# An earlier L1 tail in the head of batch 2, with its weight steps, rows and CA product moved

## The reference, cut to what matters

```
x = x + L0(x)      # L0: sum of 3 gated MLPs per batch, 256 -> 1024 -> 256: one shared, 2 chosen experts
x = x + L1(x)      # L1: one expert: down(silu(up(x)+bu) * (gate(x)+bg)) + bd, 256 -> 512 -> 256
x = x + L2(x)      # L2: x @ (sum_g y_g weight_g * mask)^T + bias
x = x + L3(x)      # L3: x @ W_base^T + b_base + 2 * (low-rank x @ A^T B^T weighted by w)
# x is (4, 512, 256): four batches of 512 rows. L0 MLP: gelu(x@g) * (x@u) @ d
```

## Time and profile before

| | |
|---|---|
| median of 3 runs | 494.5 us (494.38 to 494.57) |
| the profiled execution | 495.4 us |
| its span, first to last instruction | 493.7 us |
| mean granted TensorE clock | 0.993 |
| PE busy | 485.0 us (98%) |
| DVE busy | 376.4 us (76%) |
| ACT busy | 265.4 us (54%) |
| PE's share of the chain that ended last | 92% |

### The profile page before, as it was taken

One profiled execution on the slowest core, in us unless ns is written; L12 is line 12 of the kernel. 1 busy time (PEld: TensorE's weight loads), 2 busy tenths in 40 slices (PEclk: granted clock), 3 DMA queues, 4 the chain that ended last, 5 costly groups with the idle time before them and its releaser, 6 DMA issues.

```text
span 493.7 us, 6911 instructions
## 1 busy us (share of the span) xinstructions
PE 485.0 (98%) x2260; PEld 404.1 (82%) x2260; DVE 376.4 (76%) x647; ACT 265.4 (54%) x426; POOL 29.8 (6%) x51
## 2 busy tenths in 40 slices
PE   7999999999999999999999799999999999999997
PEld 6887888888888888888888588888888888888897
DVE  3869878977536588986987868898887577867766
ACT  4555644645446444655544646676666363636452
POOL 1820300000000200000000001000000000020000
PEclk8999999999999999999999989999999999999999
DMA  7778898258320432424380052304049220230001
GB/s 220 153 153 225 201 204 200 64 150 148 89 64 0 123 113 66 127 72 122 87 169 0 1 161 75 100 29 126 3 101 198 88 64 2 64 108 0 2 0 44
DMA packets 113812, 48.33 MB, mean 98 GB/s; under 512 B 66344, under 2 KB 112560, under 8 KB 113776
## 3 DMA queue, kind: packets, MB, share of 16 engines
q1 hardware_dynamic: 111328, 42.74, 34.6%
q0 software_dynamic: 2448, 5.15, 4.0%
HBM read 45.77 MB, written 2.10 MB: 97 GB/s over the span
## 4 chain that ended last, share of the span: by engine, by line
PE 92%; DVE 4%; ACT 1%; issue 1%; DMA 1%; SPq 0%; DVEq 0%; ACTq 0%
PE bank_a L1491 8%; PE bank_a L1492 8%; PE bank_a L1493 8%; PE bank_b L1492 8%; PE bank_b L1491 8%; PE bank_b L1493 8%; PE out L1515 6%; PE out L1519 6%; PE out L1516 6%; PE tail L1492 2%; PE tail L1493 2%; PE tail L1491 2%; PE tail L1515 2%; PE tail L1516 2%; PE tail L1519 2%; PE bank_a L1767 2%
## 5 line engine op out<-in xcount | busy, mean ns | idle before, releaser
L646 ACT ACTIVATE hid_hi<-hid 128x512 fp32r<-128x512 f32 x92 | 58.1, 632 | 93.8 <-DVE hid L905 57.2
L638 ACT ACTIVATE hid<-bank_a 128x512 f32<-128x512 f32 x80 | 47.6, 595 | 57.4 <-PE bank_a L1493 56.3
L913 DVE TENSOR_TENSOR hid_lo<-hid,hid_hi 128x512 fp32r<-128x512 f32 x92 | 63.2, 687 | 14.0 <-ACT hid_hi L646 14.0
L905 DVE SCALAR_TENSOR_TENSOR hid<-bank_b,mine,hid 128x512 f32<-128x512 f32 x64 | 47.6, 744 | 31.2 <-PE bank_b L1493 29.7
L893 DVE TENSOR_TENSOR w_lo<-raw,w_hi 128x768 fp32r<-128x768 f32 x59 | 56.0, 950 | 0.0
L1492 PE MATMUL bank_a<-x_lo,w_hi 128*128 128x512 f32 x118 | 46.0, 390 | 0.0
L1491 PE MATMUL bank_a<-x_hi,w_hi 128*128 128x512 f32 x118 | 46.0, 390 | 0.0
L1493 PE MATMUL bank_b<-x_hi,w_lo 128*128 128x512 f32 x118 | 45.9, 389 | 0.0
L1493 PE MATMUL bank_a<-x_hi,w_lo 128*128 128x512 f32 x118 | 45.9, 389 | 0.0
L1491 PE MATMUL bank_b<-x_hi,w_hi 128*128 128x512 f32 x118 | 45.9, 389 | 0.0
L1492 PE MATMUL bank_b<-x_lo,w_hi 128*128 128x512 f32 x118 | 45.9, 389 | 0.0
(11 more groups left out here) (327 smaller groups left out, 1131.9 us busy)
## 6 DMA issues: line engine op xcount, KB each, us to landing
raw<-in_L_cond_skill_gate SPq DMA_DIRECT2D x32, 256.0 KB, 2.9
raw<-in_L_cond_skill_up SPq DMA_DIRECT2D x32, 256.0 KB, 3.1
raw<-in_L_cond_skill_down SPq DMA_DIRECT2D x64, 128.0 KB, 3.2
raw<-in_L_cond_shared_down SPq DMA_DIRECT2D x22, 128.0 KB, 3.6
raw<-in_L_cond_shared_gate SPq DMA_DIRECT2D x10, 256.0 KB, 2.9
raw<-in_L_cond_shared_up SPq DMA_DIRECT2D x10, 256.0 KB, 3.3
raw_gate<-in_L_cond_W_gate SPq DMA_DIRECT2D x16, 128.0 KB, 3.2
early<-in_L_cond_weight POOLq DMA_DIRECT2D x2, 1024.0 KB, 10.7
```

The costliest lines, as they stand in the source:

```text
L638: nc.scalar.activation(hid[:, tile_of(g)], bank_a[tile_of(g)][:, :], func, **kw).then_inc(act_ready, 1)
L646: nc.scalar.activation(hid_hi[:, tile_of(g)], hid[:, tile_of(g)], ACT.Copy).then_inc(hid_hi_ready, 1)
L905: ins = nc.vector.scalar_tensor_tensor(tile, bank, weight, tile, ALU.mult, ALU.mult)
L913: nc.vector.tensor_tensor(hid_lo[:, tile], hid[:, tile], hid_hi[:, tile].bitcast(F32), ALU.subtract).then_inc(hid_lo_ready, 1)
```

## The change

L1's four chunks stand behind chunk 3 of batch 2 in place of chunk 5, and `x2` with its residual at chunk 4 in place of 6. The ten `a2` steps, two in each of the chunks 1 to 5 before, are now at chunks 1, 2, 3, 5 (two each), 6 and 7 (one each), and ACT's split of `a2` goes from chunk 6 to the end of chunk 7. The pair sums of unit 0 are formed at chunk 5 and split at chunk 6. `x4` and `output` of batch 1 go from pair unit 0 to chunk 6. Batch 2's `ca_product` goes from unit 1 (ahead of product 2) to the end of unit 0. Nothing is added and nothing taken away; batches 0, 1 and 3 keep their order.

```diff
-OUT_PLACE = 7
+OUT_PLACE = {2: 6, 3: 7}
+A_HEAD = {1: (0, 1), 2: (2, 3), 3: (4, 5), 5: (6, 7), 6: (8,), 7: (9,)}
+PAIR_SUMS_AT = 5
-L1_PLACE = {1: 5, 2: 5, 3: 4}
-X2_PLACE = {2: 6, 3: 5}
+L1_PLACE = {1: 5, 2: 3, 3: 4}
+X2_PLACE = {2: 4, 3: 5}
@@ ACT, pair_head
                     if i == X2_PLACE[PAIR]:
                         residual_hi(PAIR, 1)
+                    if i == PAIR_SUMS_AT + 1:
+                        pair_sums_hi(0)
+                    if i == MLP_CHUNKS - 1:
                         weights_split_hi(a2_hi, a2[:, :], (a2_step, A_STEPS * (PAIR + 1)))
-                    if i == MLP_CHUNKS - 1:
-                        pair_sums_hi(0)
@@ DVE, pair_unit
                 if m == 0:
                     weights_split_lo(PAIR, 2, a2_hi, a2_lo, a2[:, :])
-                    output(PAIR)
@@ DVE, pair_head
-                    if 1 <= i <= L1_PLACE[b]:
-                        a2_step_n(b, 2 * i - 2)
-                        a2_step_n(b, 2 * i - 1)
+                    for step_n in A_HEAD.get(i, ()):
+                        a2_step_n(b, step_n)
                     if i == X2_PLACE[b]:
                         x2(b, hidden_of(b, L1_PLACE[b]) + C1)
+                    if i == PAIR_SUMS_AT:
                         pair_sums(0)
-                    if i == MLP_CHUNKS - 1:
+                    if i == OUT_PLACE[b]:
+                        output(b)
+                    if i == PAIR_SUMS_AT + 1:
                         pair_sums_lo(0)
@@ PE, pair_unit
-                if m == 1:
-                    ca_product(PAIR)
                 pair_product_of(m, 4)
                 if m:
                     pair_down_of(m - 1, 0)
-                else:
-                    x4(PAIR)
                 gate_or_up(PAIR, n, 1, weights, *x_k)
@@ PE, pair_unit, its end
                 if m:
                     pair_down_of(m - 1, 1)
+                else:
+                    ca_product(PAIR)
@@ PE, pair_head
+                    if i == OUT_PLACE[b]:
+                        x4(b)
```

More of the change, by code:

```diff
@@ L1428, in pair_rest @@
                         weights_split_lo(b, 2, a2_hi, a2_lo, a2[:, :])
-                    if i == OUT_PLACE:
+                    if i == OUT_PLACE[b]:
                         output(b)
```

## The result

| | before | after |
|---|---|---|
| median, first comparison (5 runs each) | 494.38 us | 489.60 us (489.44 to 489.9) |
| ratio, 95% interval | | 0.9917, 0.9892 to 0.9941 |
| median, second comparison, on one chip (11 and 5 runs) | 493.45 us (492.3 to 494.69) | 490.60 us (489.78 to 490.94) |
| ratio, 95% interval | | 0.9939, 0.9925 to 0.9954 |
| span of the profiled execution | 493.7 us | 488.2 us |

Faster, by 4.8 us in the first comparison and 2.85 in the second, where 3.45 were forecast. The forecast was 491.0 us, with a range of 489.7 to 492.8. That the gain differs by 2 us from one comparison to the other is part of what had to be explained.

The account below looks back on a forecast made before the run. PE was taken to bound the kernel, busy 485.0 of 493.7 us. Of 5.35 us lost in batch 2's head, 1.9 would remain: gain 3.45, from 494.5 to 491.0 us, range 489.7 to 492.8.

Parts of the forecast that it names:

- The stall of chunk 7 goes, a shorter one comes at chunk 5: PE's 2.97 us stall at chunk 7's down product goes; chunk 5's down product waits on `hidden_hi`, 0.9 us lost.
- `x4` gives DVE the room in chunk 6: At chunk 6, `x4`'s 24 matmuls give DVE 2.87 us more before chunk 6's down product, with no wait.
- The second stall, ACT's copy behind `a2`'s split: Ahead of unit 0's product 2, PE waits 0.3 us for ACT's first `pair_copy`, 0.4 with the restart.
- Cover in unit 0, product 4 and 5: Unit 0 without `x4`: low copy ready 0.1 us before product 4, high sum's add 0.4 before product 5; no stall.
- The third stall, CA on `a2_lo`: End of unit 0: PE waits 0.35 us for `a2_lo` before the CA product, 0.5 with the restart.
- The loss before, 5.35 us: Kernel before, 280.7 to 300.62 us: PE time lost to the stall, slow clock and small gaps, the most to gain.
- The loss after, 1.9 us: Changed kernel's head: stalls of 0.9, 0.4 and 0.5 us, with 0.1 for product 4.
- the 0.1 for product 4: Unit 0's product 4: low copy ready at 288.85, wanted at 288.95; 0.1 us allowed in the loss.
- The clock: Behind the new short stalls: the sum counts no clock loss, granted clock 1.00 from 270 to 300 us.
- one fall after the change: Rival: one short idle lowers the clock once, costing 1.61 us; gain 1.85, 492.65 us, chance 0.11.
- "The median stood 0.9 below the profiled time": Whole kernel: step from profiled time 491.9 us, equivalently from 494.5 less 3.45, to the forecast median 491.0.
- The time behind the head: From unit 1's product 2 to the end: no PE stalls before, so the time stays the same and the gain lasts.

Follow-up runs that it names:

- the two delayed kernels: Changed kernel with two, and with four, more 128x512 DVE adds ahead of chunk 5's `hidden`: 491.98 us and 494.92 us.
- moving two steps into such gaps: Kernel before, L1 still behind chunk 5, `x4` ahead of chunk 7's down product, DVE's `output` and `a2` split moved to idle places: 490.19 us, then 489.87.
- two edits that shortened the stalls by only 0.4 us: Kernel before with `x4` moved ahead of chunk 7's down product, 491.57 us; changed kernel with `x4`, `output`, `ca_product` put back, 491.66 us.
- the kernel with `x4` first: Changed kernel with `x4` ahead of chunk 6's down product step in place of behind it: 489.69 us.
- The kernel with `x4` as cover: Kernel before with only `x4` moved, to right ahead of unit 0's down product of chunk 7: 491.57 us, ratio 0.9962.

## Why the prediction was right, point by point

The mechanism came out as written, and the sum is 0.45 us short of what the profiles give. The number 489.60 itself holds some luck of the draw, since the same kernel gave 490.60 in the second comparison.

- **The stall of chunk 7 goes, a shorter one comes at chunk 5.** Right: 0.9 forecast, 0.81 measured, on the line and in the chunk named. The added DVE work of the two delayed kernels shows its cause.
- **`x4` gives DVE the room in chunk 6.** Right: without it, 1.65 us more are lost at chunk 6, chunk 7 and product 2 than in the changed kernel.
- **The second stall, ACT's copy behind `a2`'s split.** Right in place and cause, 0.24 for 0.4. Moving the split took it away together with `x4`'s place.
- **Cover in unit 0, product 4 and 5.** Nothing, as forecast.
- **The third stall, CA on `a2_lo`.** Right, 0.40 for 0.5. That CA's cover is worth more than its wait was shown by putting it back.
- **The loss before, 5.35 us.** Right for an execution in which the clock falls behind the stall, 60 in 89, and so for the median; taken as certain because one profile had it, which was not justified. The second profile of the same kernel loses 3.7. So the change brings 3.7 - 1.45 = 2.2 us in an execution without the fall and 3.9 with it. The lowest times of all (491.5 and 489.44) are 2.1 apart; the median of the 89 (493.4) and the two medians of the changed kernel are 3.8 and 2.8 apart.
- **The loss after, 1.9 us.** The term that was mis-sized: it measured 1.45, each of the three stalls 0.1 to 0.16 shorter than written and the 0.1 for product 4 not there. With it the sum would be 3.9.
- **The clock.** I gave one fall after the change 0.11. It has none in ten executions. In five profiles of other kernels with idle times of 0.4 to 1.6 us in the head none fell either, nor in the changed kernel's two. The rule that I cited from the Trainium skill ("TensorE: Matmul & The Clock Gate", section "A second HAM failure mode: psum-queue depth-cycling"), that short idles between groups can make the clock swing, was not borne out at these lengths here; a single one of 2.0 us did lower it.
- **"The median stood 0.9 below the profiled time", and all three runs of before at 494.5.** I read three close times as a fixed value. Of 89 later executions of the kernel before 27 were under 492.5, and their median is 493.4. The profiled execution of the kernel before had a slow start besides its fall; whether the other four of the first comparison, whose median is 494.38, had one too is not on record, but 0.9 us of its 4.8 are more than the change is worth by the profiles.
- **The time behind the head.** From unit 1's product 2 to the end of the span: 193.1 us before, 193.1 after. Right.

## What to carry to other kernels

When an engine at 98% has one wait, list the work that stands in front of the late instruction on the engine that is late, and look for the nearest idle time of that engine further down: moving two steps into such gaps did here what a rebuilt schedule did. An independent block of matmuls is worth most directly ahead of the product whose operand is late, and each such block moved takes its cover from where it stood, so follow the other engines' lists through that place too. A loss that one profile shows and no instruction explains, as a low clock, has a price and a frequency: take the price from the profile and the frequency from the mean clocks of all executions. Here two edits that shortened the stalls by only 0.4 us gained 1.9, because the stall that was left was too short to bring the clock down.

## What the runs showed of the hardware that I had not expected

- The clock's answer to a stall differs between executions of one program: an idle time of 2.82 us was followed by ten matmuls at a slower pace, one of 2.84 by none. A fall followed at 2.0 and 3.4 us, none at 1.57 or below, in the profiles of the head of batch 2. By the clocks of all executions it followed 5 times in 10 (2.0 us), 60 in 89 (2.8) and 9 in 10 (3.4), at about 1.6 us each.
- The granted clock of a stretch can miss a slow spell. In the kernel with `x4` first, seven matmuls near the start began 0.43 us apart, as they do in the kernel before where the granted clock is 0.51, and the stretch around them, 7 to 10 us, has 1.00. The kernel with `x4` as cover shows the same. The distance between starts is the safer reading. The rows, and the stretch behind them:

```profile
7.33 0.63 PE L1539 MATMUL bank_b<-x_hi,res_hi 128*128 128x512 f32 x1
7.76 0.63 PE L1542 MATMUL bank_a<-x_hi,res_lo 128*128 128x512 f32 x1
```
```profile
7.00:10.00 3.00, 3.00 (x8) 1.00 0.90 277
```

- Three things differ between executions and cost 1.6 to 1.8 us each where they appear: the clock behind the long stall; the clock near 8 us, slow for some 3 us in 3 of 13 profiles (the first of the kernel before, and the two named in the point above); and batch 0's L1 weights, which DVE turned at 80.2 us in both profiles of the kernel before and between 76.2 and 78.9 in the eleven others. The late weights cost PE time in one profile only. The first of the three makes the largest groups of the times; how the other two divide what is left was not measured.
